# New slot orders on five engines, root refinement on GpSimd, half of the mask behind its scores

## The reference

```python
x = x + xattn(layernorm(x), ctx, ctx, deltas, mask, ...)
z = layernorm(x)
for i in range(6):
    z = attn_layer(shift_tokens(z), Wqkv[i], q_scale[i], k_scale[i], Wo[i]) + z
    z = ffn_layer(shift_tokens(z), ln_g[i], ln_b[i], W1[i], b1[i], W2[i], b2[i]) + z
return x + z
# attn_layer: 16 heads of 64; q and k are divided by their norm, scaled, rotated;
# windows of 32 queries see the 32 keys before and their own 32, masked, softmax, times v, times Wo
# shift_tokens: the second half of the features comes from the token before
# ffn_layer: layernorm, W1 to 2 x 341, a * gelu(gate), W2
```

## Time and profile before

| | |
|---|---|
| median of three runs | 3205.43 us |
| profiled execution | 3206.1 us, its span 3204.3 us |
| busy over the span | PE 96%, DVE 95%, ACT 86%, POOL 77% |
| granted TensorE clock, mean | 0.983 |
| DMA, share of 16 engines | 21.8% |

### The profile page before, as it was taken

How to read it: one execution, slowest core, us unless ns; L and a number is a source line. 1 busy time by engine, 2 the same in 40 slices (tenths; PEclk the granted TensorE clock), 3 DMA queues, 4 the chain that set the end, 5 groups by cost and what they waited for, 6 DMA issues and landing times.

```text
span 3204.3 us, 169944 instructions
## 1 busy us (share of the span) xinstructions
PE 3068.8 (96%) x71268; PEld 2196.2 (69%) x71268; DVE 3040.4 (95%) x6045; ACT 2739.9 (86%) x5443; POOL 2456.7 (77%) x2675
## 2 busy tenths in 40 slices
PE   6777899999999999999999999999999999999997
PEld 4444567777777777777777777777777777777775
DVE  7887889999999999999999999999999999999995
ACT  6887688888888888888888888888888888888885
POOL 3333778888888888888888888888888888888884
PEclk9888999999999999999999999999999999999998
DMA  3000221222222222222222222222212222222222
GB/s 81 7 7 6 53 53 51 61 51 81 67 55 58 52 60 72 75 52 58 54 55 78 65 61 52 61 52 76 72 51 61 51 61 79 62 58 52 60 52 60
DMA packets 150374, 182.24 MB, mean 57 GB/s; under 512 B 51572, under 2 KB 74162, under 8 KB 149554
## 3 DMA queue, kind: packets, MB, share of 16 engines
q1 hardware_dynamic: 150322, 181.55, 21.8%
HBM read 21.32 MB, written 2.10 MB: 7 GB/s over the span
## 4 chain that ended last, share of the span: by engine, by line
DVE 54%; issue 21%; PE 19%; DMA 2%; POOL 2%; DVEq 1%; SPq 1%; ACT 0%; POOLq 0%; ACTq 0%
DVE rs L1098 5%; DVE n L1123 4%; DVE hT L1078 4%; DVE P L1038 3%; DVE ta L1112 3%; DVE ta L997 3%; DVE rowmax L1021 3%; DVE ta L1047 3%; DVE tb L1050 3%; DVE sm L1085 3%; DVE P L1059 3%; DVE tb L1151 2%; DVE sm L1070 2%; PE bank L1413 2%; PE bank L1368 2%
## 5 line engine op out<-in xcount | busy, mean ns | idle before, releaser
L1070 DVE TENSOR_REDUCE sm<-sq 128x32 f32<-128x2048 f32 x192 | 436.4, 2273 | 0.0
L1413 PEld LDWEIGHTS bank<-wo,oT 128*128 128x128 f32 x3072 | 373.5, 192 | 91.2 <-issue 90.1
L1413 PE MATMUL bank<-wo,oT 128*128 128x128 f32 x3072 | 374.7, 275 | 0.4 <-ACT gl L772 0.4
L532 POOL TENSOR_TENSOR qk<-qk,rn 128x512 f32<-128x512 f32 x192 | 200.2, 1043 | 210.6 <-DVE rn L1026 210.6
L1368 PEld LDWEIGHTS bank<-PT,vs 64*64 64x64 f32 x18432 | 289.7, 136 | 91.4 <-issue 89.8
L1368 PE MATMUL bank<-PT,vs 64*64 64x32 f32 (+1 forms) x18432 | 311.8, 221 | 3.6 <-issue 3.6
L577 POOL TENSOR_TENSOR P<-P,rowsum 128x512 f32<-128x512 f32 x192 | 200.4, 1044 | 148.6 <-DVE rowsum L1105 148.6
L1441 PEld LDWEIGHTS bank<-cst,qk 32*128 32x128 f32 x12288 | 206.7, 137 | 147.7 <-issue 147.4
L1338 PEld LDWEIGHTS bank<-qkT 64*32 64x32 f32 x24576 | 277.6, 105 | 14.1 <-issue 3.9
L1338 PE MATMUL bank<-qkT 64*32 64x64 f32 x24576 | 281.1, 225 | 3.2 <-issue 3.2
L589 POOL TENSOR_TENSOR qk<-ta,tb 128x512 f32<-128x512 f32 x192 | 245.6, 1279 | 9.2 <-DVE tb L1115 9.2
(11 more groups left out here) (164 smaller groups left out, 9289.9 us busy)
## 6 DMA issues: line engine op xcount, KB each, us to landing
vs<-vt SPq DMA_DIRECT2D x1152, 128.0 KB, 2.4
wqkv<-L_ffn_Wqkv SPq DMA_DIRECT2D x6, 1024.0 KB, 5.3
zm<-zm SPq DMA_DIRECT2D x192, 31.8 KB
wqkv<-L_ffn_Wqkv SPq DMA_DIRECT2D x6, 512.0 KB, 3.9
wo<-L_ffn_Wo SPq DMA_DIRECT2D x6, 512.0 KB, 3.9
z_sb<-x SPq DMA_DIRECT2D x4, 512.0 KB, 5.2
ctxb<-ctx SPq DMA_DIRECT2D x32, 64.0 KB, 1.8
w<-L_ffn_W SPq DMA_DIRECT2D x6, 341.0 KB
```

The costliest lines, as they stand in the source:

```text
L1070: v_.tensor_reduce(sm[:, :], sq[:, :].rearrange("p (h d) -> p h d", d=DH), AX.X, ALU.add).then_inc(s["d_sumsq"], 1)
L1413: ins = t_.matmul(bank[7][:, 384:512], oT[:, c, :], wo[:, 2 * (c % 4) + c // 4, :], start=c == 0, stop=c == PAIRS - 1)
```

## The change

What it does, engine by engine:

- **TensorE**: the slot's order was zT, qk2, P transposes, scores, qk3, znT, value products, gate, v0, a, v1, y, qk0, QK transposes, y2, qk1. It becomes zT, y2, qk2, qk3, P transposes, scores, value products, znT, v0, gate, a, qk0, v1, y, qk1, QK transposes. y2 now has lag 5. Several waits become edges.
- **Scores**: the masks of windows 0 and 1 still come first (start); those of windows 2 and 3 come after the last scores of their windows (stop), and scores of windows 2 and 3 run two head pairs ahead of those of 0 and 1.
- **ScalarE**: new order zs, tr2, tr0, sq2, tr3, sq3, PT0, PT1, table, zn, AV0, v0, AV1, gelu, table, sq0, v1, exp, ln, rn, sq1, tr1. The copies tr0, tr2, tr3 have lag 2 now, tr1 keeps lag 1. The squares take over the factor 2^8, so that the sum comes scaled.
- **VectorE**: new order z, ve, rot2, rot3, zn, max1, max0, sumsq, sub1, sub0, h, clamp, rot0, zm, sum of P, reciprocal, rot1, bn_stats, bn_aggr. The clamp is a max reduction over a pair in `sm` whose second member is the constant. The three Newton operations are gone.
- **GpSimd**: does the Newton step in four operations of 128x32, each waiting for the one before, after ScalarE's `a_rn`; a factor of one half per root goes into the rotation tables. New order rstd (lag 4), add2, add1, z copy, qk3, add3, qk0, qk1, zmb (lag 4), qk2, Newton step, P1, P0, add0.
- **Sync engine**: `load_qk` in two halves with semaphores of their own; the rotation load after a `shift_v`; `load_v` behind `shift_z(end - 4)`, `load_o` behind `shift_z(end - 1)`, `load_w1` at the start of the next layer.
- **Loop**: starts at slot 8 instead of 6.

```diff
-        LOOP0, UNROLL = 6, 2
+        LOOP0, UNROLL = 8, 2
-            def load_qk(layer):
+            def load_qk(layer, j):
+                for i in (2 * j, 2 * j + 1):
+                    wait(sp, f"p_qk{i}", B * layer)
+                c = slice(INNER * j, INNER * j + INNER)
+                sp.dma_start(wqkv[:, c], Wqkv[layer, :, c]).then_inc(s[("l_wq", "l_wk")[j]], 16)
...
                 if layer > 0:
                     load_small(layer)
+                    load_w1(layer)
                     load_w2(layer)
...
                 shift_z(end - 5, 1)
-                if layer + 1 < DEPTH:
-                    load_qk(layer + 1)
+                if not last:
+                    load_qk(layer + 1, 0)
+                    load_qk(layer + 1, 1)
                 shift_v(end - 2, 0)
-                if layer + 1 < DEPTH:
+                if not last:
+                    load_rot(layer + 1)
+                shift_z(end - 4, 0)
+                if not last:
                     load_v(layer + 1)
-                shift_z(end - 4, 0)
                 shift_v(end - 1, 1)
...
                 shift_z(end - 1, 1)
-                if layer + 1 < DEPTH:
+                if not last:
+                    load_o(layer + 1)
+                    shift_v(end + 2, 0)
                     load_b2(layer + 1)
-                    shift_v(end + 2, 0)
-                    load_w1(layer + 1)
...
+                u, on, p = unit(n, k, 0)
+                if on:
+                    wait(pool, "a_rn", done(u))
+                    edge(pool, u, "d_nr0", done(u))
+                    r_ = rn[:, p, :]
+                    g.tensor_tensor(n0[:, :], sc[:, :], r_, ALU.mult).then_inc(s["g_n0"], 1)
+                    wait(pool, "g_n0", done(u))
+                    g.tensor_tensor(n1[:, :], n0[:, :], r_, ALU.mult).then_inc(s["g_n1"], 1)
+                    wait(pool, "g_n1", done(u))
+                    g.tensor_tensor(n2[:, :], three[:, 0:1].to_broadcast([128, 2 * HEADS]), n1[:, :], ALU.subtract).then_inc(s["g_n2"], 1)
+                    wait(pool, "g_n2", done(u))
+                    g.tensor_tensor(r_, r_, n2[:, :], ALU.mult).then_inc(s["g_rn"], 1)
...
-                    v_.scalar_tensor_tensor(sm[:, :], sm[:, :], NORM_MIN2, sm[:, :], ALU.max, ALU.max).then_inc(s["d_nr0"], 1)
+                    v_.tensor_reduce(sc[:, :], sm[:, :, :], AX.X, ALU.max).then_inc(s["d_nr0"], 1)
...
-                    v_.scalar_tensor_tensor(n0[:, :], sm[:, :], -0.5 * LN_UP, rn[:, p, :], ALU.mult, ALU.mult).then_inc(s["d_nr1"], 1)
...
+                    for w in (0, 1):
+                        mask(w, True)
+                    for c in range(2):
+                        for w in (2, 3):
+                            score(w, c, c == 0)
                     for c in range(PAIRS):
-                        for w in range(4):
-                            for e in range(2):
-                                dr = slice(64 * e, 64 * e + 64)
-                                k0 = WIN * max(w - 1, 0)
-                                ins = t_.matmul(SC[e][32 * w:32 * w + 32, 64 * c:64 * c + 64],
-                                                qkT[dr, c, 32 * w:32 * w + 32], qkT[dr, PAIRS + c, k0:k0 + 64],
-                                                start=False, stop=c == PAIRS - 1, skip_group_check=True)
+                        for w in (0, 1):
+                            ins = score(w, c, False)
+                        if c + 2 < PAIRS:
+                            for w in (2, 3):
+                                score(w, c + 2, False)
+                        if c + 3 == PAIRS:
+                            for w in (2, 3):
+                                mask(w, False)
                     ins.then_inc(s["p_S"], 1)
```

More of the change, by code:

```diff
@@ L404, in _ @@
                 start, end = B * layer, B * layer + B
+                last = layer + 1 == DEPTH
                 if layer == 0:
@@ L525, in slot @@
             def slot(n, k):
+                u, on, p = unit(n, k, 4)
+                if on:
+                    wait(pool, "d_ve", done(u))
+                    g.tensor_tensor(rstd[:, p:p + 1], ve[:, p:p + 1], half_neg[:, 0:1], ALU.pow).then_inc(s["g_rstd"], 1)
+                u, on, p = unit(n, k, 0)
+                if on:
+                    wait(pool, "d_rot2", done(u))
+                    edge(pool, u, "p_tr", done(u - 2))
+                    g.tensor_tensor(qk[:, p, 1024:1536], ta[:, 1024:1536], tb[:, 1024:1536], ALU.add).then_inc(s["g_add2"], 1)
@@ new lines, in slot @@
+                u, on, p = unit(n, k, 0)
+                if on:
+                    edge(pool, u, "d_rot1", done(u))
+                    edge(pool, u, "p_tr", done(u - 2))
+                    g.tensor_tensor(qk[:, p, 512:1024], ta[:, 512:1024], tb[:, 512:1024], ALU.add).then_inc(s["g_add1"], 1)
+                u, on, p = unit(n, k, -3)
+                if on:
+                    edge(pool, u, "p_zT", done(u - 2))
+                    wait(pool, "z_ready", u + 1)
+                    g.tensor_copy(zcur[:, p, :], z_sb[:, cols(u)]).then_inc(s["g_z"], 1)
@@ new lines, in slot @@
+                u, on, p = unit(n, k, 1)
+                if on:
+                    edge(pool, u, "g_add1", done(u))
+                    edge(pool, u, "g_rn", done(u))
+                    q3 = qk[:, p, 512:1024].rearrange("p (h d) -> p h d", d=DH)
+                    g.tensor_tensor(q3, q3, rn[:, p, 8:16].unsqueeze(2).to_broadcast([128, 8, DH]), ALU.mult).then_inc(s["g_qk1"], 1)
+                u, on, p = unit(n, k, 4)
+                if on:
+                    edge(pool, u, "d_zm", done(u))
+                    edge(pool, u, "z_ready", done(u - 2) + B if not (isinstance(u, int) and u - 2 < 0) else 0)
+                    wait(pool, "l_b2", 16 * layer_of(u) + 16)
+                    g.tensor_tensor(zmb[:, p, :].rearrange("p (c e) -> p c e", c=2), zm[:, p, 0:3:2, :],
+                                    b2r[:, :].rearrange("p (c e) -> p c e", c=2), ALU.add).then_inc(s["g_zmb"], 1)
@@ L990, in slot @@
             def slot(n, k):
+                u, on, p = unit(n, k, 5)
+                if on:
+                    wait(dve, "p_y2", done(u))
+                    edge(dve, u, "g_zmb", done(u))
+                    v_.tensor_tensor(z_sb[:, cols(u)], bank[6][:, 384:512], zmb[:, p, :], ALU.add).then_inc(s["z_ready"], 1)
+                u, on, p = unit(n, k, 4)
+                if on:
+                    wait(dve, "d_agg", done(u))
+                    v_.tensor_scalar(ve[:, p:p + 1], mv[:, 1:2], LN_EPS, None, ALU.add).then_inc(s["d_ve"], 1)
                 u, on, p = unit(n, k, 0)
@@ L1341, in slot @@
[L1341 to L1354 removed]
+                            ins = t_.matmul(SC[e][32 * w:32 * w + 32, :], selb[dr, i:i + 32],
+                                            maskb[dr, :].unsqueeze(1).to_broadcast([64, PAIRS, DH]),
+                                            start=start, stop=not start, skip_group_check=True)
@@ new lines, in score @@
+                    def score(w, c, start):
+                        for e in range(2):
+                            dr = slice(64 * e, 64 * e + 64)
+                            k0 = WIN * max(w - 1, 0)
+                            ins = t_.matmul(SC[e][32 * w:32 * w + 32, 64 * c:64 * c + 64],
+                                            qkT[dr, c, 32 * w:32 * w + 32], qkT[dr, PAIRS + c, k0:k0 + 64],
+                                            start=start, stop=w < 2 and c == PAIRS - 1, skip_group_check=True)
+                        return ins
@@ L1375, in slot @@
                 if on:
-                    wait(pe, "a_zn", done(u))
-                    edge(pe, u, "a_zs", done(u + 5))
-                    wait(pe, "l_w1", 16 * layer_of(u) + 16)
-                    for j, (o, m_) in enumerate(FCH):
-                        ins = t_.matmul(bank[7][0:m_, 128 * j:128 * j + 128], w1[:, FF + o:FF + o + m_], znT[:, :], start=True, stop=True)
-                    ins.then_inc(s["p_gate"], 1)
+                    wait(pe, "d_zn", done(u))
+                    edge(pe, u, "z_ready", done(u - 1) + B if not (isinstance(u, int) and u - 1 < 0) else 0)
+                    t_.transpose(bank[6][:, 0:128], zn[:, :], ident).then_inc(s["p_znT"], 1)
                 u, on, p = unit(n, k, 0)
@@ L1391, in slot @@
                 if on:
+                    wait(pe, "a_zn", done(u))
+                    edge(pe, u, "a_zs", done(u + 5))
+                    wait(pe, "l_w1", 16 * layer_of(u) + 16)
+                    for j, (o, m_) in enumerate(FCH):
+                        ins = t_.matmul(bank[7][0:m_, 128 * j:128 * j + 128], w1[:, FF + o:FF + o + m_], znT[:, :], start=True, stop=True)
+                    ins.then_inc(s["p_gate"], 1)
+                u, on, p = unit(n, k, 4)
+                if on:
                     edge(pe, u, "a_zn", done(u))
-                    wait(pe, "l_w1", 16 * layer_of(u) + 16)
                     for j, (o, m_) in enumerate(FCH):
```

361 lines of the change are left out of this document (152 added, 209 removed), and 9 rows, old and new, of the table names.

## The result

The changed kernel takes 3212.2 us against 3204.9 us (medians of 20 runs each); the ratio is 1.0022, 95% interval 1.0015 to 1.0029. It is slower by 0.2%, where 3155 us were forecast, and outside the range of 3110 to 3195. The profiled execution of the changed kernel took 3207.5 us, its span is 3205.7 us at the same mean clock (0.983); that is 1.4 us more span than before.

The account below looks back on a forecast made before the run. TensorE was taken as the bound. Slots of 14.42 instead of 14.66 over 182 loop slots save 43.7 us, the queue 11, and the loop start costs 4: 3206.1 to 3155 us, range 3110 to 3195.

Parts of the forecast that it names:

- The bound: TensorE bounds the loop, a slot being a sum of its stretches; VectorE's 98.5% holds some 1.4 us of waiting.
- Value products to the slot's end: TensorE's stretch from the value products to the end of the slot stays at 9.54 us.
- Order on TensorE: Two tiled excursions instead of three save 0.09 and 0.10 us, giving 14.47 us a slot.
- Half the mask behind the scores: On TensorE, late masks of windows 2 and 3 hide 0 to 0.23 us; by itself 14.24 to 14.47 a slot.
- Rival A: On TensorE the mask is not hidden, scores run at their issue rate: slots of 14.53, 3175 us; chance 0.20.
- ScalarE's floor: ScalarE's copies up to PT1 take 4.82 us before the value products, setting a slot floor of 14.36.
- Roots on GpSimd: Newton step moves from VectorE to GpSimd, which reaches 13.5 us a slot; P0 stays hidden with 0.35 us spare.
- c: Time of GpSimd's four dependent 128x32 operations together: 1.2 to 2.4 us, taken as 1.35.
- rival C: GpSimd's chain with the roots becomes the bound: c = 2.4, slots of 14.95, 3252 us; chance 0.12.
- Queue: Sync engine's reordered loads end TensorE's idle time at layer changes: worth 5 to 14 us, taken as 11.
- Loop start and tail: Two more straight-code slots cost 2 to 10 us, taken as 4; the lag of 5 adds at most 1 at the tail.
- D: A loop not seen (zn, sq1 or rot1) takes the 0.24 back: slots of 14.66, 3199 us; chance 0.08.

Follow-up runs that it names:

- the kernel of 3163.7 us: Changed kernel with v1 split around gate, QK transposes first in body, tr3 before sq2, VectorE statistics first, zmb after qk2; 0.9877 of the kernel before.
- slots of 14.37: The kernel of 3163.7 us with all masks ahead of the scores again and the loop from slot 6; 3156.7 us, 0.9854 of the kernel before.

## Why the prediction was wrong

- **The bound** was right: TensorE, a slot as a sum of stretches. VectorE's 98.5% did hold waiting: without L1123 and L1085 it is busy 13.0 us a slot instead of 14.4, though not the 12 that were forecast. That freeing it alone would save nothing was not run.
- **The sum of the slot, term by term.** Scores start: 3.38 forecast, 3.39 measured. Masks and scores: 1.50 (what 14.42 leaves), measured 1.62. Value products to the slot's end: 9.54, measured 9.63. So two terms failed, the hiding of the mask by 0.12 and the rest of the slot by 0.09, and together they are the 0.22 between 14.42 and 14.64. In the 9.63 a gain and two losses are added up, as the next point says.
- **Order on TensorE.** The price of tiled excursions was right and even low. In the kernel of 3163.7 us the stretches add up to 14.38; against before, three whole-array stretches are 0.10 shorter each (gate 0.77 to 0.66, y2 0.77 to 0.67, qk2 0.955 to 0.86) and the other small differences nearly cancel: -0.28 in all, where -0.19 was counted. The failing step here is "from the value products to the slot's end stays": it took every stretch behind the scores as undisturbed. Two were not. The gate product lost its cover, since the value products no longer stand between it and the transpose of zn (+0.135), and the transposes went last in the body, where the branch shows (+0.08). The first could be read from the trace of before: ScalarE's copy of zn takes 0.45 plus hand-overs, v0 only 0.86, and nothing but v0 was left between. The branch behind the transposes no row of before shows, since there it lies behind a product of 512 columns.
- **Half the mask behind the scores.** Rival A's mechanism, "scores run at their issue rate", is what happened: 1.62. The argument of 10.9 ns a score was in the text, and the value was still taken near the other end. The prediction gave it 0.20; by the forecast's own sum it is worth 0.11 a slot (14.53 for 14.42), the largest single step between forecast and measurement.
- **ScalarE's floor.** The start of the scores behind tr3 (0.06) was right, measured 0.05 on average, and 0.10 in each slot with the branch moved. PT1 was never late, and in slots of 14.37 TensorE doesn't wait for it: the floor of 14.36 is not contradicted. But the same list of ScalarE steps was not followed to sq2, rot2, GpSimd and back to the transposes. In the changed kernel that loop is 14.2 and, with VectorE's branch in it, 14.75 in turn: even with the stretches as forecast the slot could not have been 14.42 in both parities. (For what TensorE needs of P0 the prediction counts with 2.68 in one place and 2.85 in another and doesn't say why; nothing hangs on it, since P is never late.)
- **Roots on GpSimd.** c is 0.25 x 4 and 0.08 between: 1.23 (forecast 1.35). P is in time in the loop; rival C is out.
- **Queue.** 8 us gained against 11, inside 5 to 14. "All moved loads are wanted half a slot or more after they can be issued" was wrong for rot, which is late by up to 1.2. That b2 had to move because zmb did was not seen: the prediction looked for new entries behind the QK load alone. That the new queue order holds b2 further back was luck for this term: with the old order the new lag costs 30 us.
- **Loop start and tail.** +4 and at most 1 were forecast. The start was sized right: the QK transposes of the first unit are 1.3 us later than before, those of the tenth 3.5. The tail was sized far too low: from the QK transposes of the fifth unit from the end the kernel takes 7.3 us more (111.4 instead of 104.1), with waits for issue of up to 1.8 us in the value products, gate products that wait for znT, and a granted clock of 0.85 instead of 0.91 (3110 to 3190 us). Why the tail stalls more than before was not tried.
- **The sum** of the trace: -2 (loop), -8 (layer changes), +3.5 and +7.3, together +1 us, as the spans say (+1.4). Of the 57 us between the forecast and the median, 42 are the slots, 3 the queue, 7 the tail, and 5 lie between the profiled run and the median. In the loop, TensorE's own 14.38 would have given (14.655 - 14.38) x 182 = 50 us; the gate took back 0.135 x 182 = 25, the branch 15, tr3 9.
- **Rivals.** D, a loop not seen, came nearest in time (3199) and held 0.08; that it lay near was luck, since its three named places (zn, sq1, rot1) were not it in the changed kernel. A regression by lost cover on the bound engine itself was not among the rivals at all.

## To carry to other kernels

When a group moves on the engine that bounds, go through each producer and consumer pair on it that another engine serves, and ask what work still lies between the two; a move that saves a mode change is easily paid back by a cover of 1.5 us that shrinks to 0.9. Follow each cross-engine loop once around and add it up: it is the next floor, and an edit on it can be worth nothing until the first one is lowered (here 0 us, then 23). Look as well whether an edit that frees one wait lengthens such a loop. Put the end of a loop's body behind a long instruction, as TensorE shows here, or inside a wait that the engine has anyway, as VectorE does.

## Seen in the hardware

- TensorE's compare-and-branch takes 208 ns (median of 91) against 45 on ScalarE and GpSimd and 56 on VectorE; it shows as 0.16 us behind 64 transposes and as nothing behind 512 columns. On VectorE the turn of the loop showed as 0.56.
- 128 score instructions: 1.39 us with 64 columns, 1.21 with 32.
- Of the 136 matmuls of masks and scores the first 32 start early and the 33rd 0.41 us behind the first, whatever the order of masks and scores or the width of the scores; from there they start 10.2 ns apart (8.7 with 32 columns).
- A product of 512 columns cut in two of 256 took 0.43 + 0.43 us, no more than the whole (0.86).
- Four dependent 128x32 operations on GpSimd: 0.25 each, 0.08 between.
